# Graph network, two layers: the source half of the hh edge weights goes through high and low halves instead of plain FP32 matmuls

## What is computed

```python
feat = jnp.concatenate([n_f[edge_src], n_f[edge_dst]], axis=1)
e_hh = jax.nn.relu(feat[:E_HH] @ W_hh + b_hh)                  # the first 128 edges
e_oo = jax.nn.relu(feat[E_HH:E_HH + E_OO] @ W_oo + b_oo)       # the next 640
e_ho = jax.nn.relu(feat[E_HH + E_OO:] @ W_ho + b_ho)           # the other 7424
logit = (jnp.concatenate([e_hh, e_oo, e_ho]) @ W_a + b_a)[:, 0]
```

## Time and profile before

| | us |
|---|---|
| median of 3 runs | 357.74 |
| lowest and highest | 357.41, 359.77 |
| the profiled execution, its own time | 357.13 |
| its span, first to last instruction | 355.0 |
| PE busy | 321.2 (90%) |
| DVE busy | 290.1 (82%) |
| ACT busy | 195.3 (55%) |
| POOL busy | 113.3 (32%) |

### The profile page before, as it was taken

One profiled execution on the slowest core, in us unless ns is written; L12 is line 12 of the kernel. 1 busy time (PEld: TensorE's weight loads), 2 busy tenths in 40 slices (PEclk: granted clock), 3 DMA queues, 4 the chain that ended last, 5 costly groups with the idle time before them and its releaser, 6 DMA issues.

```text
span 355.0 us, 4630 instructions
## 1 busy us (share of the span) xinstructions
PE 321.2 (90%) x1440; PEld 248.6 (70%) x1440; DVE 290.1 (82%) x416; ACT 195.3 (55%) x300; POOL 113.3 (32%) x125
## 2 busy tenths in 40 slices
PE   2889999999999999799999999999899997799480
PEld 1768887776644787588888888878686775588230
DVE  0799999986789979699999999978879879656535
ACT  2754396212043333788988888536157677352255
POOL 4300052074000830079999999600000000050000
PEclk9999999999999999899999999999999999699696
DMA  6999499879998994003030000023698994000003
GB/s 228 401 402 374 162 308 413 256 252 235 298 353 298 368 378 178 2 0 118 3 120 0 2 3 1 2 59 118 192 350 276 346 330 164 0 2 1 0 0 118
DMA packets 17638, 63.10 MB, mean 178 GB/s; under 512 B 2234, under 2 KB 2236, under 8 KB 17360
## 3 DMA queue, kind: packets, MB, share of 16 engines
q1 hardware_dynamic: 13520, 50.07, 39.2%
q0 software_dynamic: 2096, 8.74, 8.4%
q10 hardware_dynamic: 2000, 4.00, 3.5%
HBM read 59.64 MB, written 3.16 MB: 177 GB/s over the span
## 4 chain that ended last, share of the span: by engine, by line
PE 67%; DVE 22%; ACT 5%; issue 3%; DMA 2%; SPq 0%; DVEq 0%; ACTq 0%
PE ps L1318 21%; PE ps L1165 11%; PE ps L1209 8%; PE ps L1415 7%; DVE W_lo L735 6%; PE ps L1352 4%; PE ps L1325 3%; PE ps L1184 3%; PE ps L1360 2%; DMA x_nat<-in_x_dram 2%; PE ps L1385 2%; PE ps L1441 2%; DVE tile_val L755 1%; PE ps L1241 1%; PE ps L1223 1%
## 5 line engine op out<-in xcount | busy, mean ns | idle before, releaser
L469 ACT CAST W_hi<-W_raw 128x1024 fp32r<-128x1024 f32 x66 | 67.4, 1046 | 59.6 <-DMA W_raw<-in_L_gnn_W_ho_dram 24.4
L972 DVE SCALAR_TENSOR_TENSOR ps<-ps,wa_bc 128x1024 f32<-128x1024 f32 x74 | 87.6, 1256 | 2.7 <-PE ps L1318 2.7
L735 DVE TENSOR_TENSOR W_lo<-W_raw,W_hi 128x1024 fp32r<-128x1024 f32 x62 | 74.1, 1223 | 13.0 <-ACT W_hi L469 9.7
L1318 PE MATMUL ps<-A_tab,oh 128*128 x148 | 53.9, 445 | 2.4 <-ACT oh L575 2.4
L1165 PE MATMUL ps<-W_hi,xT_hi 128*128 128x512 f32 x112 | 46.4, 415 | 0.7 <-DVE W_lo L735 0.7
L1318 PE MATMUL ps<-B_tab,oh 128*128 x148 | 46.9, 398 | 0.0
L1165 PE MATMUL ps<-W_lo,xT_hi 128*128 128x512 f32 x112 | 44.2, 395 | 0.0
L1165 PE MATMUL ps<-W_hi,xT_lo 128*128 128x512 f32 x112 | 34.9, 393 | 0.0
L425 POOL TENSOR_SCALAR sc<-sc 128x256 f32<-128x256 f32 x37 | 32.7, 883 | 3.3
L423 POOL TENSOR_TENSOR sc<-irow,keys 128x256 f32<-128x256 f32 x37 | 23.6, 639 | 27.9 <-PE ps L1325 27.6
L1318 PEld LDWEIGHTS ps<-B_tab,oh 128*128 128x128 f32 x148 | 28.4, 192 | 5.5
(11 more groups left out here) (255 smaller groups left out, 556.4 us busy)
## 6 DMA issues: line engine op xcount, KB each, us to landing
W_raw<-in_L_gnn_W_oo_dram SPq DMA_DIRECT2D x8, 1024.0 KB, 9.8
W_raw<-in_L_gnn_W_ho_dram SPq DMA_DIRECT2D x8, 1024.0 KB, 5.4
W_raw<-in_L_gnn_W_hh_dram SPq DMA_DIRECT2D x8, 1024.0 KB, 8.4
W_raw<-in_L_gnn_W_hn_dram SPq DMA_DIRECT2D x8, 1024.0 KB, 5.7
W_raw<-in_L_gnn_W_on_dram SPq DMA_DIRECT2D x8, 1024.0 KB, 6.9
W_raw<-in_L_gnn_W_dram SPq DMA_DIRECT2D x4, 1024.0 KB, 7.1
key_rows<-key_rows_scratch POOLq DMA_DIRECT2D x1, 2304.0 KB, 14.2
table_scratch<-tabs ACTq DMA_DIRECT2D x2, 1024.0 KB, 6.5
```

The lines of the kernel that those rows point to most:

```text
L469: sa.copy(halves(n)[0], W_raw[:, n // 2 % NS, n % 2, :]).then_inc(hi_made, 1)
L735: v.tensor_tensor(lo, W_raw[:, n // 2 % NS, n % 2, :], hi.bitcast(F32), ALU.subtract).then_inc(lo_made, 1)
L972: v.scalar_tensor_tensor(acc, acc, 0.0, wa_bc[:], ALU.max, ALU.mult, accum_out=keys[:, t, 2:3]).then_inc(reduced, 1)
L1318: ins = mm(acc[:, n * 512:(n + 1) * 512], oh[:, t // 2 % 2, k, t % 2 * P:(t % 2 + 1) * P], tab[:].rearrange("p q d -> p (q d)")[:, n * 512 ...
```

## The change

Chunks 18, 19, 22, 23, 26, 27, 30 and 31 become split chunks. ACT casts them and DVE makes their low halves; PE uses six fp32r matmuls for each instead of two plain ones. The transposed source features are split too: ACT copies G0's first 1024 columns as fp32r into `hh_hi`, DVE subtracts into a new tile `hh_lo`. The target half (chunks 32 to 39) stays plain. The pairs of `W_raw` with the eight chunks become free by DVE's low halves. The rings `W_hi` and `W_lo` keep four chunks and now count these eight too. `hh_lo` takes the place of `cle` in one memory region, and `cle` moves to another.

```diff
         def split(n):
-            return chunks[n][0] != "hh"
+            return chunks[n][0] != "hh" or chunks[n][1] < KC
...
-            sa.copy(hh_x[:].rearrange("p k c n -> p (k c n)"), G0).then_inc(act_step, 1)
+            sa.copy(hh_hi[:].rearrange("p c n -> p (c n)"), G0[:, 0:D])
+            sa.copy(hh_x[:].rearrange("p c n -> p (c n)"), G0[:, D:2 * D]).then_inc(act_step, 1)
...
-            for n in (17, 20, 21):
+            for n in (17, 18, 19):
                 high(n)
...
-            for n in (24, 25, 28, 29):
+            for n in range(20, 32):
                 high(n)
...
-            lows(8, 10)
+            low(8)
+            dve.wait_ge(act_step, act_at("hh_x"))
+            link(v.tensor_tensor(hh_lo[:].rearrange("p c n -> p (c n)"), G0[:, 0:D],
+                                 hh_hi[:].rearrange("p c n -> p (c n)").bitcast(F32), ALU.subtract))
+            stage("hh_lo")
+            low(9)
...
-            low(17)
+            lows(17, 20)
             tiles_of(1)
             low(20)
             low(21)
             dve.wait_ge(pe_step, pe_at("perm0"))
             tile_values(1, 0)
             tile_values(1, 1)
+            low(22)
+            low(23)
             positions_of(1)
...
             stage("key_u8")
-            low(28)
-            low(29)
+            lows(26, 32)
             dve.wait_ge(act_step, act_at("C_hh"))
...
-                    pe.wait_ge(w_in[n // 2 % NS], 16 * (n // 2 // NS + 1))
-                    for f in range(0, D, 512):
-                        ins = mm(G0[:, f:f + 512], hh_x[:, row // KC, row % KC, :],
-                                 W_raw[:, n // 2 % NS, n % 2, f:f + 512], start=(row == 0), stop=(row == 2 * KC - 1))
+                    if split(n):
+                        W1, W0 = split_chunk(n)
+                        for part, Ws in ((hh_hi, (W1, W0)), (hh_lo, (W1,))):
+                            for f in range(0, D, 512):
+                                for W in Ws:
+                                    ins = mm(G0[:, f:f + 512], part[:, row, :], W[:, f:f + 512],
+                                             start=(row == 0 and part is hh_hi and W is W1), stop=False)
+                    else:
+                        pe.wait_ge(w_in[n // 2 % NS], 16 * (n // 2 // NS + 1))
+                        for f in range(0, D, 512):
+                            ins = mm(G0[:, f:f + 512], hh_x[:, row % KC, :], W_raw[:, n // 2 % NS, n % 2, f:f + 512],
+                                     start=False, stop=(row == 2 * KC - 1))
                     ins.then_inc(chunk_used, 1)
...
-            pe.wait_ge(act_step, act_at("hh_x"))
+            pe.wait_ge(dve_step, dve_at("hh_lo"))
             x_dense(END["ooA"], END["ooB"], G0)
```

More of the change, by code:

```diff
@@ L95, in gnn_two_layers @@
         cum = sb("cum", [P, NC, JH], F32, before_ends)
+        cle = sb("cle", [P, NT, NC], BF16, before_ends)
         before_ends.close()
@@ L108, in gnn_two_layers @@
         before_sums = ExitStack()
+        hh_lo = sb("hh_lo", [P, KC, P], F32R, before_sums)
         place_no = sb("place_no", [P, P, JS], BF16, before_sums)
-        cle = sb("cle", [P, NT, NC], BF16, before_sums)
         before_sums.close()
@@ L131, in gnn_two_layers @@
         before_halves = ExitStack()
-        hh_x = sb("hh_x", [P, 2, KC, P], F32, before_halves)
+        hh_hi = sb("hh_hi", [P, KC, P], F32R, before_halves)
+        hh_x = sb("hh_x", [P, KC, P], F32, before_halves)
         before_halves.close()
@@ L302, in gnn_two_layers @@
                       "exp0", "exp1", "h_relu0", "h_exp0", "h_exp1", "h_relu1", "h_exp2", "h_relu2", "sd2", "sd3", "out3"]
-        DVE_STAGES = ["xT0", "xT1", "tot", "totals", "columns", "ooA_out", "placed0", "placed1", "keys", "key_u8", "hoA_b",
+        DVE_STAGES = ["xT0", "xT1", "tot", "totals", "hh_lo", "columns", "ooA_out", "placed0", "placed1", "keys", "key_u8", "hoA_b",
                       "hoA_lo", "hoB_lo", "maxima", "P", "PT", "zT0", "parts",
```

## The result

The changed kernel takes 371.11 us, the median of 4 runs (370.02 to 372.45); the kernel before, on the same chip, 357.69 us (357.41 to 359.77). The ratio is 1.038 with a 95% interval of 1.0343 to 1.0416: slower by 13.4 us. The forecast was 368.0 with a range up to 371.0: the sign and the order of the waits came as forecast, the size fell short by 3.1 us and the time lies just above the range. The four executions form two pairs, 370.02 and 370.15 us at a mean granted clock of 0.955, 372.07 and 372.45 us at 0.951, and the profiled one (372.07, span 370.0, 15.0 more than before) is of the longer pair.

A forecast was written before the change was run, and what follows sets the result against it. The prediction took PE as first bound with DVE just under it, and the change as moving work to DVE. The profiled 357.13 us plus a shift of 10.85 (+9.3 at chunk 40, +1.5 clock) gave 368.0; range 362.5 to 371.0.

The forecast's parts named there:

- step 5: At chunk 40: PE waits 6.4 us, starts at 125.25 instead of 115.91 (+9.3); clock loss of 1.5 makes +10.8.
- step 4: From the bias of ho (109.5): DVE has 15.75 us of work without a wait, so low(40) ends at 125.25.
- Step 1: Up to chunk 14: hh_lo on DVE delays the chain by 1.15 us; PE starts chunk 14 at 56.1.
- Step 2: At perm(1): low halves delay positions_of(1); PE waits 3 us, until 80.85 instead of 77.35 (+3.5).
- Step 3: Behind the wait at perm(1): PE's clock drops to half for 3 us, losing 1.5 us.
- Step 4, the ring,: Four-place W_hi: high(30), high(31) wait for PE's use of 26, 27; DVE is free at 99.3, not 85.89 (+13.4).
- Step 6: Behind chunk 40: the shift stays unchanged to the end; earlier weight transfers are worth nothing.
- no loss by the clock: Rival: PE's clock stays full behind its waits; DVE leads, 366.3 us; chance 0.17.
- the ring doesn't bind: Rival: high(31) never waits for PE in the four-place ring, so PE loses 4.7: 361.9 us; chance 0.08.
- PE alone decides: Rival: new DVE work fits its idle time, PE keeps 2.9 less 1.15: 355.4 us, faster; chance 0.03.
- Half hidden: Rival: all of DVE's idle time is filled and landings are kind: 358.5 us, within 1%; chance 0.04.

The follow-up runs named there:

- e2: The kernel before with only hh_hi and hh_lo made and all hh chunks left plain: 359.08 us, ratio 1.0038.
- e5: The changed kernel with low(22) and low(23) behind positions_of(1) on DVE instead of ahead of it: 368.71 us, ratio 1.0305.
- e12: The kernel before with only chunks 22, 23, 26, 27 split, a late 512-column hh_lo, positions_of(1) before low(22), POOL's copies behind low(41): 360.85 us, ratio 1.0096.
- e3: The changed kernel with low halves 28 to 31 spread behind the shares on DVE, and ACT's count copies ahead of high(28) and high(30): 364.61 us, ratio 1.0219.
- e7: The changed kernel with POOL's copies of x's transpose waiting for low(41) instead of PE's use of chunk 39: 369.57 us, ratio 1.0338.
- e4: The changed kernel with 24 unused matmuls on PE while it waits at chunk 40: 368.26 us, ratio 1.0318.
- e9: The kernel before with source hh chunks as six fast matmuls on ready operands (product left out), and POOL's copies behind low(41): 356.14 us, ratio 0.9963.
- e1: The kernel before with source hh chunks as six fast matmuls on ready operands, nothing added for DVE or ACT (product left out): 361.07 us, 12 runs.
- e10: The changed kernel with low halves 18, 19, 26, 27, 30, 31 made by POOL, and orders mended at positions_of(1), count copies and POOL's copies: 369.42 us, ratio 1.033.
- e6: The changed kernel with low(28) to low(31) spread behind the shares, positions_of(1) before low(22), and POOL's copies behind low(41): 361.34 us, ratio 1.0124.
- e13: e12 with casts 28, 29 behind the count copies on ACT and their low halves behind the first shares on DVE: 359.6 us, ratio 1.0061.

## Where the prediction was wrong, and what it had right

Two terms failed: step 5's "The clock is down again: +1.5", which measured 2.7 us, and the last sentence of step 4, 15.75 us of work from the bias of ho to low(40), which took 16.7 since POOL, to which the prediction gave no term, now ran beside it. The sign and the chain were right: PE waits for pos_oh, then the ring holds DVE, then PE waits for low(40), with the clock down behind both. The 15.0 us of the span against the 10.85 forecast come apart by the steps:

- **Step 1** held: hh_lo cost 1.4 us by itself (e2), forecast 1.15; its own row is 1.22. In the changed kernel chunk 14 starts at 56.67, forecast 56.1.
- **Step 2** held: perm(1) at 81.34, forecast 80.85; the wait 2.92, forecast 3. Undone, it gave back 2.4 us (e5). The 0.5 us more is that of step 1.
- **Step 3** held: 29 matmuls in 3.56 instead of 1.96, 1.6 us, forecast 1.5.
- **Step 4, the ring,** held in its result: shares at 99.90 (forecast 99.3), bias of ho at 110.08 (109.5). Its account of the ring was too narrow. It let only 30 and 31 wait; 28 and 29 waited too, for 24 and 25. In the changed kernel the last wait covers that; in e12, built on the same thought, it moved the shares but not chunk 40. Undone, the ring's part was the largest, 6.5 us (e3). (27 used at 96.85, a cast of 1.05 and a low half of 1.23 make 99.13, where the step says 99.3; nothing hangs on it.)
- **Step 4, "From there to the end of low(40) DVE had 15.75 us of work",** failed by 1 us: it took 16.7, because POOL's copies of x_both and the work behind them, released by PE, now ran beside DVE's last instructions. The prediction spoke of POOL nowhere. Without that overlap chunk 40 starts 1.0 us earlier (e7).
- **Step 5, "The clock is down again: +1.5",** is the term that was mis-sized most: chunk 40 took 5.46 instead of 2.74, 2.7 us. The prediction took the 3 us at half clock behind the first gather for every fall, and allowed 2 at most; behind 7.4 us of waiting the clock was down for 5.5 us. With the wait filled, chunk 40 took 2.86 (e4). The 2.7 is that of one execution: behind waits of 6.47 and 9.96 us chunk 40 took 4.48 (e7) and 4.60 (e5), which is 1.7 and 1.9 us more than before and near the top that the prediction allowed.
- **Step 6** held to the first gather (+13.8 there as at chunk 40). The other 1.2 us of this execution's span lie behind it, in two stretches of layer 1 in which the same matmuls ran at a lower granted clock: twelve took 5.37 us at 318.35 where they took 4.48 at 304.80 before (a granted clock of 0.53 and 0.65), eight took 6.30 at 348.90 where they took 5.79 at 334.44 (0.58 and 0.64). In e5 and e7 the twelve took 4.74 and 4.67, so most of this is the one execution's own.

The shortfall of 4.15 is then 0.6 carried from steps 1 to 4, 1.0 by POOL, 0.1 from the end of low(40) to PE's start, 1.2 by the clock at chunk 40 and 1.2 behind the first gather. The range had room for the clock (0.5 more for each fall), but not for the clock and POOL together. These parts are read from one execution of the longer pair; the shorter pair, at 370.1, was not profiled.

Of the rivals, "no loss by the clock" fell by the windows and by e4, "the ring doesn't bind" by ACT's waits and by e3. "PE alone decides" would have needed 355.4: the kernel that gives PE its gain and DVE nothing measures 356.1 (e9), the real change 371.1. The Trainium skill, "Perfetto Trace Analysis", section Identifying the Most-Contended Engine, says to optimise first the engine with the highest occupancy, but for TensorE it calls the busy share of matmuls a poor measure and names MFU (the share of the peak arithmetic rate that is used) and the busy share of weight loads in its place. By the weight loads PE is at 70% and DVE, at 82%, stands ahead of it; the runs agree with that reading, since what was given to DVE set the time. No run here gives MFU. "Half hidden" put the change at 358.5; even the best order tried stands at 361.3.

Of the 13.4 us, then: 6.5 by the ring, 2.4 by the order at perm(1), 1.5 by POOL, each undone alone, and 4.1 that stay with all three undone. These add up to 14.5; each of these medians is uncertain by about 1 us, so that the 1.1 too much says nothing, and only the ring's part is clear by the times alone. The clock is no fifth part: its falls stand behind these waits and are inside the other numbers.

## What to carry to other kernels

Before work is moved from the busiest engine to the next one, add up that engine's idle time between here and the next place where the first waits for it, and compare with the work moved: 10.35 us into 7.7 was lost in every order tried. Then follow every buffer ring the new work enters (each entry waits for the use that many entries back, its neighbours' too), since an in-order queue passes that wait on to all behind it. Look for the wait that ends next: taking the ring's wait out of e12 gave nothing at chunk 40, since the gathered rows came no earlier. When a fast engine gets faster, look at what its progress releases on a third engine, and what that runs beside.

## What the runs showed of the hardware that was not expected

- POOL slows DVE far more than their rows apart would say: a pair of low halves 5.42 us beside POOL's copies and the work behind them, 2.36 alone (e1, e9); a 128x74 tensor_scalar 2.40 instead of 0.19, a 128x512 one 5.99 instead of 0.42 beside POOL's subtractions (e10). Not every overlap does it: in e9 POOL's copies ran from 115.24 on beside DVE's L864 and L865, which read PSUM, and these took their usual 1.23 and 1.22 (by the section of the Trainium skill named above, an operation of DVE with at most one input in SBUF, outside certain modes, does not contend; the rows agree).
- A wait of TensorE of the same length does not always cost the same clock. Behind waits of 0.68 to 1.91 us (e1, e4, e5, e6, e9, e12, e13) it stayed at full; behind 2.2 to 3.5 us it fell in most executions, for 3 to 4 us (before, first gather; the change, perm(1)) or 6 (e12), and stayed full in some (2.89 at perm(1) in e4, 3.29 at 102.55 in e10, 2.31 at the first gather in e6); behind 4.27 us (e10) and 6.5 us and more (the change, e5, e7) it fell each time. A longer wait did not mean a larger loss behind it: behind 7.36 us chunk 40 took 5.46, behind 9.96 us 4.60. What decides within the middle group these runs leave open. It is worth up to 2.7 us at chunk 40, as much as several of the effects measured here.
